# A graph-layer kernel: high and low second-layer weights streamed as two 256-column products into one set of PSUM columns

## What is computed

```
h = jnp.maximum(_layernorm(x, axis=-1), 0.0)
agg = segment_sum(edge_features, tgt, num_segments=N_NODES)
agg = agg / jnp.maximum(counts, 1.0)[:, None]
combined = jnp.concatenate([agg, h], axis=1)
hid = jax.nn.relu(combined @ W1 + b1)      # W1: 320 x 512
out = x + (hid @ W2 + b2)                  # W2: 512 x 256
```

## Time and profile before

| | |
|---|---|
| median of three runs | 1390.73 us |
| lowest and highest run | 1389.94 and 1390.91 us |
| span of the profiled execution | 1387.8 us |
| TensorE, weight loads, VectorE busy | 1356.9, 1099.1, 1276.5 us |
| ScalarE, GpSimd busy | 818.9, 727.1 us |

### The profile page before, as it was taken

The page is one execution under the profiler, slowest core; times in us unless marked ns, Lnnn a source line. Parts: engine busy times, 40 slices in busy tenths (PEclk is TensorE's granted clock), DMA queues, the critical chain, the costliest instruction groups (busy, mean ns, idle before and its releaser), DMA issues.

```text
span 1387.8 us, 31376 instructions
## 1 busy us (share of the span) xinstructions
PE 1356.9 (98%) x6882; PEld 1099.1 (79%) x6882; DVE 1276.5 (92%) x3267; ACT 818.9 (59%) x1672; POOL 727.1 (52%) x1004
## 2 busy tenths in 40 slices
PE   3899999999999999999999999999999999999998
PEld 1688888888888888888888888888888888888887
DVE  6789999999999999999999999999999999999996
ACT  3556565656566565656565656565666656565653
POOL 4554545555555555554545454555555555555451
PEclk7999999999999999999999999999999999999999
DMA  5575757576666666575757575766666666757572
GB/s 101 104 142 107 144 107 139 110 137 112 134 114 132 117 130 124 122 132 114 142 105 144 107 140 109 137 112 135 113 133 116 131 120 126 130 116 137 109 129 56
DMA packets 424646, 168.87 MB, mean 122 GB/s; under 512 B 323181, under 2 KB 424247, under 8 KB 424633
## 3 DMA queue, kind: packets, MB, share of 16 engines
q1 hardware_dynamic: 421348, 166.77, 62.7%
q10 hardware_dynamic: 3284, 1.97, 0.8%
HBM read 66.07 MB, written 51.20 MB: 85 GB/s over the span
## 4 chain that ended last, share of the span: by engine, by line
PE 97%; DVE 1%; DMA 1%; ACT 0%; POOL 0%; issue 0%; ACTq 0%; DVEq 0%; POOLq 0%
PE P L852 26%; PE P L832 13%; PE P L854 13%; PE P L834 13%; PE P L833 13%; PE P L842 7%; PE P L841 7%; PE PS L811 3%; PE PA L821 2%; DVE below L627 1%; DMA HQ<-HN 0%; DMA dst_a<-in_dst_dram 0%; DVE HT L667 0%; ACTq L256 0%; ACT HN L514 0%
## 5 line engine op out<-in xcount | busy, mean ns | idle before, releaser
L852 PE MATMUL P<-w_both,H_hi 128*128 128x512 f32 x1568 | 566.7, 399 | 0.1
L550 ACT ACTIVATE H_hi<-P 128x512 fp32r<-128x512 f32 x392 | 234.8, 599 | 381.1 <-PE P L842 380.5
L854 PE MATMUL P<-w_both,H_lo 128*128 128x256 f32 x1568 | 438.1, 279 | 0.0
L852 PEld LDWEIGHTS P<-w_both,H_hi 128*128 128x128 f32 x1568 | 294.3, 188 | 67.3 <-DVE H_lo L684 0.5
L832 PE MATMUL P<-HT_hi,w_hi 128*128 128x512 f32 x784 | 325.7, 415 | 16.4 <-DVE HT_lo L675 16.4
L406 POOL TENSOR_TENSOR XB<-X,b_row 128x1024 f32<-128x1024 f32 x98 | 235.0, 2398 | 198.3 <-DVE O L695 198.3
L834 PE MATMUL P<-HT_hi,w_lo 128*128 128x512 f32 x784 | 311.0, 397 | 0.0
L833 PE MATMUL P<-HT_lo,w_hi 128*128 128x512 f32 x784 | 310.6, 396 | 0.0
L684 DVE SCALAR_TENSOR_TENSOR H_lo<-P,H_hi 128x512 fp32r<-128x512 f32 x392 | 268.7, 686 | 32.6 <-ACT H_hi L550 19.7
L854 PEld LDWEIGHTS P<-w_both,H_lo 128*128 128x128 f32 x1568 | 294.5, 188 | 4.2
L667 DVE STREAM_TRANSPOSE HT<-HQ 128x512 f32<-128x512 f32 x196 | 212.7, 1086 | 18.4 <-DMA HQ<-HN 18.1
(11 more groups left out here) (73 smaller groups left out, 1512.4 us busy)
## 6 DMA issues: line engine op xcount, KB each, us to landing
X<-in_x_dram SPq DMA_DIRECT2D x98, 512.0 KB, 4.5
HQ<-HN SPq DMA_DIRECT2D x388, 128.0 KB, 4.1
out_dram<-O SPq DMA_DIRECT2D x97, 512.0 KB, 4.4
ER<-in_edge_attr_dram SPq DMA_DIRECT2D x392, 32.0 KB, 1.8
DW<-in_dst_dram SPq DMA_DIRECT2D x392, 0.5 KB, 1.9
w_raw<-in_L_gnn_W_dram ACTq DMA_DIRECT2D x4, 128.0 KB, 7.6
w_raw<-in_L_gnn_W_dram ACTq DMA_DIRECT2D x2, 256.0 KB, 8.2
HQ<-HN ACTq DMA_DIRECT2D x4, 128.0 KB, 4.8
```

The lines of the kernel that those rows point to most:

```text
L550: act.activation(H1_hi[:, m, :], bank(m)[:], ACT.Relu).then_inc(s_1hi, 1)
L852: pe.matmul(out_bank(j)[:], H1_hi[:, m, rows], w2_both[:, m, :, :].rearrange("p a d -> p (a d)"), start=(m == 0), stop=False)
L854: last = pe.matmul(out_bank(j)[:, 0:D], H1_lo[:, m, rows], w2_both[:, m, 0, :], start=False, stop=(m == CH - 1))
```

## The change

Line 852's product of 512 columns becomes two of 256 columns with the same stationary block, first the high and then the low weights, and both are summed into columns 0 to 255 of the bank; columns 256 to 511 are no longer written. VectorE's `residual` then has one addition for each block, of the bank's columns 0 to 255 and `XB` into `O`; the addition into `XB`, the semaphore `s_half` and the wait on it are gone. The lines of the changed file are three or four lower in number.

```diff
@@ residual (VectorE)
-                dve.tensor_tensor(XB[b][:, j, :], out_bank(j)[:, D:2 * D], XB[b][:, j, :], ALU.add).then_inc(s_half, 1)
-                dve.wait_ge(s_half, SUB * t + j + 1)
                 dve.tensor_tensor(O[b][:, j, :], out_bank(j)[:, 0:D], XB[b][:, j, :], ALU.add).then_inc(s_fin, 1)
@@ layer2 (TensorE)
-                        pe.matmul(out_bank(j)[:], H1_hi[:, m, rows], w2_both[:, m, :, :].rearrange("p a d -> p (a d)"),
-                                  start=(m == 0), stop=False)
+                        pe.matmul(out_bank(j)[:, 0:D], H1_hi[:, m, rows], w2_both[:, m, 0, :], start=(m == 0), stop=False)
+                        pe.matmul(out_bank(j)[:, 0:D], H1_hi[:, m, rows], w2_both[:, m, 1, :], start=False, stop=False)
                         last = pe.matmul(out_bank(j)[:, 0:D], H1_lo[:, m, rows], w2_both[:, m, 0, :],
                                          start=False, stop=(m == CH - 1))
```

More of the change, by code:

```diff
@@ L232, in build @@
         s_l2 = sem("s_l2")
-        s_half = sem("s_half")
         s_fin = sem("s_fin")
```

## The result

The changed kernel takes 1404.36 us (median of four runs, 1404.19 to 1404.58) against 1390.82 us before: +13.5 us, ratio 1.0099 with a 95% interval of 1.0085 to 1.0112. The forecast was 1395.8 us, slower by 5.1 us, with a range up to 1400.0 us. The direction was right; the size and the range were wrong.

What follows compares the result with a forecast made beforehand. The prediction took TensorE's instruction stream as the bound, plus start-up and tail. 1390.73 us before, + 5.5 for the split, 0 for loads, - 0.46 for one addition in the tail, gave 1395.8 us; range 1390.0 to 1400.0 us.

Steps and rivals of the forecast that it cites:

- What bounds the kernel: From the second tile on, TensorE's instruction stream sets the time; nothing VectorE does ends a wait of TensorE.
- VectorE's busy time: 392 additions of 419 ns go, 164.1 us of busy time, leaving VectorE near 1112 us busy.
- The tail: After the last product one addition follows instead of two, so the end comes 0.46 us sooner.
- The wide product split: Second layer: three 256-column products take 353.1 ns against a pair's 349.6 ns, 1568 times: +5.5 us, bounds +2.0 to +7.6.
- The loads at nothing: The 1568 added stationary loads, 113 ns apart, hide under 256-column products of 117.7 ns and cost nothing.
- The rival on the loads: Loads in a row bound the narrow products from a 117.7 ns period on; at 125 ns +39.8 us, 1430 us; chance 0.10.
- The choice of row: Line 854's 117.7 ns, also fp32r with a 128 by 128 load following, taken for all three narrow products.
- The far end of the load rival: Added loads stand wholly in the open, 1568 x 113 ns, +177 us, 1572 us in all; chance less than 0.01.
- the likeliest case: The split costs its fixed part: 1395.8 us, chance 0.70, of which some 0.07 falls inside 0.2%.
- The range: Eight in ten: 1390.0 us, from the no-cost rival, to 1400.0 us, 2 us above the split term's upper bound.

Runs made afterwards that it cites:

- VectorE's part by itself: Kernel before without VectorE's addition from columns 256 to 511, the wide product kept; 1390.4 us, ratio 0.9997.
- `c_half_loads`: Changed kernel with 64 of 128 stationary columns in each group's second product and, in hidden groups 0 to 2, the third; 1395.82 us, ratio 1.0038.
- the 128-column products: Changed kernel with each of a group's three products cut in two of 128 columns, each with its own load; one run, 1887.38 us.
- `i_quarter`: Kernel before with the wide product split in hidden group 1 alone, halves in separate columns, VectorE adding twice; 1395.05 us, ratio 1.0033.
- `f_grouped`: Kernel before with the same products reordered, a block's hidden groups' wide products first, then its narrow ones; 1396.81 us, ratio 1.0042.
- The bf16 run: Changed kernel with each group's second product replaced by a bf16 one of constants, 256 columns of zeros; 1407.69 us, ratio 1.0118.

## Why the prediction was wrong, point by point

**What bounds the kernel.** Right: TensorE's stream, and it alone. No wait appeared in the loop (the two of the first tile are 1.2 us together), the clock stayed at 1.00, and VectorE's part by itself gave 0.9997. VectorE's busy time was misjudged, 1062.6 us where 1112 us was forecast, without effect on the time.

**The tail.** Right by mechanism: one addition stands behind the last product, and the two splits with and without it differ by 0.4 us (1404.76 and 1404.36), though the runs scatter by as much.

**The wide product split, +5.5 us.** The fixed part of a product is there: before, over the whole trace, a narrow product takes 118.0 ns and a pair 350.3 ns, so that three narrow ones are 3.7 ns more, 5.8 us in all. With the loads relieved the changed kernel's stream runs at 117.8 ns and its time is 1395.82 us, where 1395.8 us was forecast for the changed kernel. This term was right for products whose loads are covered. That the two times agree to 0.1 us is luck in part, since the runs of `c_half_loads` scatter by 1.6 us.

**The loads at nothing.** This is the step that failed. The prediction said: "I cost the loads at nothing; their cover is the 256-column product above them, with 4 to 5 ns to spare." The load's 113 ns, read off four loads about the transposes, was about right (111.7 ns sustained, with the 128-column products). But 6 ns to spare is not free: in a run of narrow products each takes 120.0 ns, 2.0 ns above line 854's 118.0 ns over the whole trace, three times a group, 1568 x 6.0 = 9.4 us; what the half loads gave back is 8.5 us. With the 5.8 us of the fixed part that is the 14.9 us of the longer span to 0.3 us. The rival on the loads had the cause but treated it as a threshold, "it decides from a period of 117.7 ns on", and so gave it nothing at 111.7 ns and 40 us at 125 ns. What was measured lies between, as an excess below the threshold.

**The choice of row.** Line 854's 117.7 ns was taken as the nearest row because type, width and following load agreed. Its neighbours did not: before, every narrow product had a wide one on either side, so that away from the transposes the distances between loads were 0.12 and 0.23 us in turn, never 0.12 us twice running:

```profile
1202.30 0.19 PEld L854 LDWEIGHTS P<-w_both,H_lo 128*128 128x128 f32 x1
1202.54 0.19 PEld L852 LDWEIGHTS P<-w_both,H_hi 128*128 128x128 f32 x1
1202.65 0.19 PEld L854 LDWEIGHTS P<-w_both,H_lo 128*128 128x128 f32 x1
```

One split group between wide products (`i_quarter`) is enough to take 361.0 ns. In `f_grouped`, where nothing is split, block 2's four narrow ones take 120 ns each, block 3's 118 ns over the whole trace.

**Small slips in the prediction's numbers.** The far end of the load rival, the forecast of 1395.8 us and 177.2 us, is 1573 us and not 1572. The part of the likeliest case within 0.2% is 0.07 in one sentence and 0.06 in the sum behind it. Neither bears on the outcome.

**The range** reached 2 us above the term's upper bound for "a fixed part slightly larger in a row of three". It should have run to what three narrow products may cost when a resource next to them is at 95% of its period (111.7 of 117.7 ns; by the prediction's own 113 ns it was 96%).

**The Trainium skill on loads.** The Trainium skill ("TensorE: Matmul & The Clock Gate", LDWEIGHTS (loading the stationary operand)) gives a load as its columns over 1.2 GHz, 107 ns for 128, whatever the rows. The trace's 111.7 ns in a row of loads is near it. The Trainium skill's rule on the same page (The mechanism) that loads overlap products only in other row groups doesn't hold in this trace: three loads of 111.7 ns and three products of 118.0 ns, all of the same 128 rows, share 360 ns.

**What stays open.** By what mechanism loads that follow one another every 111.7 ns make a product of 118.0 ns late is not shown. That narrower loads remove the excess, and that 8 more columns remove two thirds of it, is. Whether the 111.7 ns belong to the load itself or to another limit on an fp32r load with its product no run separates. The bf16 run, a miss for MARGIN, has only an argued explanation. Most of the loss of `f_grouped`, in wide products and outside the second layer, has none. No version tried is clearly faster than the kernel before: of VectorE's additions, the only thing the change saves, one alone is on the path.

## What to carry to other kernels

On a stream of TensorE products that never waits, relief for VectorE is worth nothing and each extra product is worth its fixed part and its load. Here fp32r loads of 128 by 128 follow one another every 111.7 ns at best, so products of 256 columns (118 ns) are at the edge: alone between wide ones they cost nothing extra, in a row 120 ns each, and at 264 columns 0.6 ns of the excess is left. When a term rests on the nearest row, compare the row's neighbours as well as its form, and don't count as hidden what fills nearly all of its cover, as 111.7 ns did of 118.

## What was not expected of the hardware

- Two overlapped streams of 111.7 and 118 ns a piece gave 120.0 ns, more than either.
- The order of the same wide and narrow products is worth 5.9 us: 1396.81 us with the wide ones first, against 1390.96. Only 1.4 us of it is in the narrow ones.
- A bf16 load behind an fp32r product started 0.11 us after that product, beside its own product, and not at once as fp32r loads do; a kernel with a third of its second-layer products in bf16 was slower than the all-fp32r one, 1407.69 against 1404.36 us.
- With VectorE's 392 additions gone, two small instructions of each tile took less than half of their time before: 158 ns in place of 511, and 161 in place of 324.
